# An attention and feed-forward kernel: its 32-bit transposes on half the rows of TensorE

## What is computed

```python
xn = layernorm(x)                                        # x: 32, 256, 128
q, k, v = (einsum('bsd,hde->bhse', xn, w) + b for ...)   # 16 heads of 8
scores = softmax(einsum('bhse,bhte->bhst', q, k) * scale)
att = einsum('bhst,bhte->bhse', scores, v)
attention = att.reshape(b, s, 128) @ wo.T + bo
xr = mu_r * xn + (1 - mu_r) * xn_prev;  xk = mu_k * xn + (1 - mu_k) * xn_prev
r = sigmoid(xr @ W_r.T);  k_act = square(relu(xk @ W_k.T))
return x + attention + r * (k_act @ W_v.T)
```

## Time and profile before

| | us |
|---|---|
| median of 3 runs | 471.02 |
| lowest, highest | 470.27, 473.52 |
| the profiled execution | 472.43 |
| its span, first to last instruction | 469.9 |

### The profile page before, as it was taken

The page is one execution under the profiler, slowest core; times in us unless marked ns, Lnnn a source line. Parts: engine busy times, 40 slices in busy tenths (PEclk is TensorE's granted clock), DMA queues, the critical chain, the costliest instruction groups (busy, mean ns, idle before and its releaser), DMA issues.

```text
span 469.9 us, 15674 instructions
## 1 busy us (share of the span) xinstructions
PE 449.4 (96%) x5254; PEld 271.8 (58%) x5254; DVE 400.6 (85%) x824; ACT 390.7 (83%) x865; POOL 366.8 (78%) x674
## 2 busy tenths in 40 slices
PE   5598999999999999999999999999999999999996
PEld 4245665655666565666665656566656665666553
DVE  7478999988999999899998999899998999989831
ACT  2037989988988998988989899889998989898883
POOL 6568788888888888788888888888888888887321
PEclk9559999999999999999999999999999999999999
DMA  4543455544355454344554544355545444455100
GB/s 140 133 122 94 137 155 147 145 127 127 116 150 158 141 141 141 101 138 139 149 158 125 158 132 124 109 144 158 157 133 139 137 124 126 136 151 147 49 15 22
DMA packets 85836, 60.42 MB, mean 129 GB/s; under 512 B 6192, under 2 KB 73392, under 8 KB 85808
## 3 DMA queue, kind: packets, MB, share of 16 engines
q1 hardware_dynamic: 85808, 60.06, 45.0%
HBM read 29.89 MB, written 29.36 MB: 126 GB/s over the span
## 4 chain that ended last, share of the span: by engine, by line
PE 89%; DVE 4%; issue 2%; ACT 2%; DMA 1%; ACTq 0%; DVEq 0%; SPq 0%; POOL 0%; POOLq 0%
PE bank_val L605 26%; PE bank_exp L663 19%; PE bank_max L673 10%; PE misc L744 4%; PE misc L692 4%; PE misc L714 4%; PE misc L628 3%; PE misc L703 3%; PE misc L749 3%; PE misc L756 3%; PE misc L631 2%; DVE neg_max L533 2%; PE misc L726 2%; PE misc L721 1%; PE misc L613 1%
## 5 line engine op out<-in xcount | busy, mean ns | idle before, releaser
L533 DVE TENSOR_REDUCE neg_max<-bank_max 128x2 f32<-128x512 f32 x512 | 327.7, 684 | 41.5 <-PE bank_max L673 36.1
L434 ACT ACTIVATE probs<-bank_exp 128x512 f32<-128x512 f32 x504 | 272.9, 596 | 27.1 <-PE bank_exp L663 26.9
L673 PE MATMUL bank_max<-ops 48*128 48x256 bf16 x1024 | 164.1, 278 | 0.0
L663 PE MATMUL bank_exp<-ops 51*128 51x256 bf16 x1008 | 158.5, 273 | 4.6 <-issue 3.0
L605 PE MATMUL bank_val<-probs,val 128*25 128x256 f32 x2048 | 136.3, 384 | 1.4 <-ACT probs L434 1.4
L663 PEld LDWEIGHTS bank_exp<-ops 51*128 51x128 bf16 x1008 | 72.7, 95 | 71.6 <-issue 47.4
L605 PEld LDWEIGHTS bank_val<-probs,val 128*25 128x25 f32 x2048 | 50.4, 103 | 52.1 <-issue 26.1
L673 PEld LDWEIGHTS bank_max<-ops 48*128 48x128 bf16 x1024 | 75.1, 96 | 5.2
L344 POOL TENSOR_SCALAR xn<-x_in,moments,rstd 128x128 f32<-128x128 f32 x62 | 49.3, 803 | 0.0
L383 POOL TENSOR_TENSOR mixed_x<-mixed_x,xn_t 128x512 f32<-128x512 f32 x32 | 40.7, 1273 | 2.5
L358 POOL TENSOR_TENSOR qk_l<-qk_rest,qk_m 128x512 bf16<-128x512 f32 x31 | 36.1, 1164 | 2.5
(11 more groups left out here) (73 smaller groups left out, 619.5 us busy)
## 6 DMA issues: line engine op xcount, KB each, us to landing
ops<-spill SPq DMA_DIRECT2D x128, 192.0 KB, 3.4
spill<-qk_h SPq DMA_DIRECT2D x64, 192.0 KB, 3.4
spill<-qk_m SPq DMA_DIRECT2D x64, 128.0 KB, 1.9
x_in<-x SPq DMA_DIRECT2D x32, 128.0 KB, 2.2
spill<-qk_l SPq DMA_DIRECT2D x32, 128.0 KB, 1.8
y_out<-y SPq DMA_DIRECT2D x32, 128.0 KB, 1.9
ops<-shift SPq DMA_DIRECT2D x128, 6.0 KB
w<-weights SPq DMA_DIRECT2D x1, 448.0 KB, 3.0
```

What stands on the lines that cost most here:

```text
L434: nc.scalar.activation(probs[g % 2][:, u % G, :, :], exp_bank(u, live)[:, :, :], ACT.Exp, scale=SCALE).then_inc(exp_done[u], 1)
L533: nc.vector.tensor_reduce(out=neg_max[hf][:, :, r, pr], in_=bank_max[MAX_BANK[v]][:, :, :], axis=AX_X, op=ALU.max, negate=True).then_inc(m ...
L663: exp_mm = nc.tensor.matmul(exp_bank(u, live)[:, i, :], ops[p][rows, hf, 1, pr, i * P:(i + 1) * P], ops[p][rows, hf, 0, pr, :], start=True ...
L673: max_mm = nc.tensor.matmul(bank_max[MAX_BANK[v]][:, i, :], of[rows, max_hf, 0, max_pr, i * P:(i + 1) * P], of[rows, max_hf, 1, max_pr, :] ...
```

## The change

Three groups of fp32 transposes (tokens, xn, att) are cut in two: the lower 64 rows of the data and an identity of 64 x 64 give 64 columns in `misc[:, 0]`, the upper 64 rows give 64 columns in `misc[:, 1]`. Each group has twice as many matmuls, alternating between the halves. The two banks are now one tensor of two banks; the tokens lie in the second half of both, and so do xn and att. As each group writes both banks, and no two engines may use one bank at a time, the readers and writers wait for more: the gate's Tanh for the tokens, VectorE's `inv_den` for the Tanh, the xn_t copy for ffn, xn and att, L613 for xn_t as well as att_t.

Waits of TensorE are drawn forward, ahead of the gate (the second `qk_rest`, `projected`), ahead of the gate's second matmul (`mixed`) and ahead of the ffn matmuls (`xn`, `att`). VectorE makes `inv_den` and `att` behind u = 4 instead of u = 5. ScalarE copies `att_t` behind u = 8 instead of u = 7 and `projected` behind u = 12 instead of u = 11. The rows of the output weights are permuted to the new order of `att`.

```diff
-        misc = [psum(f"misc{i}", [P, 2 * S]) for i in range(2)]
+
+        misc = psum("misc", [P, 2, 2 * S])
...
                         act.wait_ge(gate_psum, n(0))
+                        after(act, tokens_psum[0], n(-1))
+                        after(act, tokens_psum[1], n(-1))
                         after(act, ffn_done, n(-1))
 
                         nc.scalar.activation(gate[:, :], near[:, 0:S], ACT.Tanh, scale=0.5).then_inc(gate_done, 1)
...
+                    if u == 7 and (live(3) or live(-1)):
+
+                        after(act, ffn_psum, n(0))
+                        for r in range(2):
+                            after(act, xn_t_psum[r], n(3))
+                            after(act, att_t_psum[r], n(-1))
                     if u == 7 and live(3):
-                        act.wait_ge(xn_t_psum, n(3))
-                        nc.scalar.copy(xn_t[(c + 3) % TURN][:, 1:1 + S], near[:, S:2 * S]).then_inc(xn_t_done, 1)
-                    if u == 7 and live(-1):
-                        act.wait_ge(att_t_psum, n(-1))
+                        nc.scalar.copy(by_rows_of_tokens(xn_t[(c + 3) % TURN][:, 1:1 + S]),
+                                       misc[:, :, S:S + P].rearrange("p r (n c) -> p r n c", c=RG)).then_inc(xn_t_done, 1)
+                    if u == 8 and live(-1):
                         after(act, wo_psum, n(-2))
-                        nc.scalar.activation(att_t[:, :], far[:, 0:S], ACT.Identity,
+                        nc.scalar.activation(by_rows_of_tokens(att_t[:, :]),
+                                             misc[:, :, S + P:2 * S].rearrange("p r (n c) -> p r n c", c=RG), ACT.Identity,
                                              bias=col[:, C_BV:C_BV + 1]).then_inc(att_t_done, 1)
...
-                    if u == 11 and live(-1) and live(0):
+                    if u == 12 and live(-1) and live(0):
...
-                    if u == 5 and live(-1):
-                        dve.wait_ge(tokens_psum, n(-1))
-                        nc.vector.reciprocal(inv_den[:, :], by_head[:, :, E]).then_inc(inv_done, 1)
+                    if u == 4 and live(-1):
+                        dve.wait_ge(tokens_psum[0], n(-1))
+                        dve.wait_ge(tokens_psum[1], n(-1))
+                        after(dve, gate_done, n(0))
+                        nc.vector.reciprocal(inv_den[:, :, :], by_head[:, :, :, E]).then_inc(inv_done, 1)
                         dve.wait_ge(inv_done, n(-1))
-                        after(dve, att_t_psum, n(-2))
-                        nc.vector.tensor_tensor(att[:, :, :], by_head[:, :, 0:E],
-                                                inv_den[:, :].unsqueeze(2).broadcast_to([P, ST * H, E]),
+                        after(dve, att_t_psum[0], n(-2))
+                        after(dve, att_t_psum[1], n(-2))
+                        nc.vector.tensor_tensor(att[:, :, :, :].rearrange("p k r e -> p r k e"), by_head[:, :, :, 0:E],
+                                                inv_den[:, :, :].unsqueeze(3).broadcast_to([P, 2, H, E]),
                                                 ALU.mult).then_inc(att_done, 1)
...
                     if u == 3 and live(0):
                         pe.wait_ge(shift_done[1], n(0))
+                        after(pe, qk_rest_done[0], n(2))
+                        after(pe, wo_done, n(-2))
                         for i in range(ST):
+                            if i == ST - 1:
+
+                                after(pe, mixed_done, n(-1))
                             last = nc.tensor.matmul(near[:, i * D:(i + 1) * D],
                                                     mixed_x[p][:, 0, i * P:(i + 1) * P], w[:, W_R, :],
                                                     start=True, stop=True)
                         last.then_inc(gate_psum, 1)
                     if u == 3 and live(-1):
-                        pe.wait_ge(mixed_done, n(-1))
-                        after(pe, qk_rest_done[0], n(2))
-                        after(pe, wo_done, n(-2))
+                        if not live(0):
+                            pe.wait_ge(mixed_done, n(-1))
+                            pe.wait_ge(wo_done, n(-2))
+                            pe.wait_ge(att_t_done, n(-2))
                         for st in range(ST):
                             for i in range(2):
-                                k = ST * st + i
-                                last = nc.tensor.transpose(far[:, k * P:(k + 1) * P],
-                                                           mixed[:, i, st * P:(st + 1) * P], ident[:, :])
-                        last.then_inc(tokens_psum, 1)
+                                k = S + (ST * st + i) * RG
+                                for r in range(2):
+                                    rows = slice(RG * r, RG * (r + 1))
+                                    last = nc.tensor.transpose(misc[:, r, k:k + RG], mixed[rows, i, st * P:(st + 1) * P],
+                                                               ident[rows, rows])
+                                    if st == ST - 1 and i == 1:
+                                        last.then_inc(tokens_psum[r], 1)
...
+                    if u == 7 and live(3):
+                        pe.wait_ge(xn_done, n(3))
+                        after(pe, qk_rest_done[0], n(2))
+                        after(pe, qk_rest_done[1], n(2))
+                    if u == 7 and live(-1):
+                        pe.wait_ge(att_done, n(-1))
...
                     if u == 7 and live(3):
-                        pe.wait_ge(xn_done, n(3))
-                        after(pe, qk_rest_done[1], n(2))
                         for i in range(ST):
-                            last = nc.tensor.transpose(near[:, S + i * P:S + (i + 1) * P], xn[:, i, :], ident[:, :])
-                        last.then_inc(xn_t_psum, 1)
+                            for r in range(2):
+                                rows, k = slice(RG * r, RG * (r + 1)), S + i * RG
+                                last = nc.tensor.transpose(misc[:, r, k:k + RG], xn[rows, i, :], ident[rows, rows])
+                                if i == ST - 1:
+                                    last.then_inc(xn_t_psum[r], 1)
                     if u == 7 and live(-1):
-                        pe.wait_ge(att_done, n(-1))
                         for st in range(ST):
-                            last = nc.tensor.transpose(far[:, st * P:(st + 1) * P],
-                                                       att[:, st * H:(st + 1) * H].rearrange("p k e -> p (k e)"),
-                                                       ident[:, :])
-                        last.then_inc(att_t_psum, 1)
+                            for r in range(2):
+                                rows, k = slice(RG * r, RG * (r + 1)), S + P + st * RG
+                                of = att[rows, st * HALF:(st + 1) * HALF].rearrange("p k r e -> p (k r e)")
+                                last = nc.tensor.transpose(misc[:, r, k:k + RG], of, ident[rows, rows])
+                                if st == ST - 1:
+                                    last.then_inc(att_t_psum[r], 1)
...
                         after(pe, att_t_done, n(-1))
+                        after(pe, xn_t_done, n(3))
```

More of the change, by code:

```diff
@@ L120, in split_attention_ffn_kernel @@
         mixed = sb("mixed", [P, 2, S])
-        inv_den = sb("inv_den", [P, ST * H])
-        att = sb("att", [P, ST * H, E])
+        inv_den = sb("inv_den", [P, 2, H])
+        att = sb("att", [P, H, 2, E])
         att_t = sb("att_t", [P, S])
@@ L156, in split_attention_ffn_kernel @@
         tables_in = sem("tables_in")
-        xn_done, xn_t_psum, xn_t_done = sem("xn_done"), sem("xn_t_psum"), sem("xn_t_done")
+        xn_done, xn_t_done = sem("xn_done"), sem("xn_t_done")
+        xn_t_psum = [sem(f"xn_t_psum{r}") for r in range(2)]
         qk_psum = [sem(f"{a}_psum") for a in "qk"]
@@ L176, in split_attention_ffn_kernel @@
         mix_psum = [sem(f"mix_psum{g}") for g in range(NG)]
[L177 removed]
+        mixed_done, tokens_psum = sem("mixed_done"), [sem(f"tokens_psum{r}") for r in range(2)]
         inv_done, att_done = sem("inv_done"), sem("att_done")
[L179 removed]
+        att_t_done, wo_psum = sem("att_t_done"), sem("wo_psum")
+        att_t_psum = [sem(f"att_t_psum{r}") for r in range(2)]
         wo_done = sem("wo_done")
@@ L333, in step @@
                     pool.wait_ge(rstd_done, n(3))
-                    after(pool, xn_t_psum, n(2))
+                    after(pool, xn_t_psum[0], n(2))
+                    after(pool, xn_t_psum[1], n(2))
                 if live(2):
@@ L556, in step @@
                         after(dve, xn_t_done, n(3))
+                        after(dve, att_t_done, n(-1))
                         after(dve, rest_done, n(-1))
@@ L587, in _ @@
             for _ in range(WARM):
-                nc.tensor.matmul(misc[0][:, 0:P], ident[:, :], ident[:, :], start=True, stop=True)
```

(1 more changed line is left out.)

21 lines of the change are left out of this document (12 added, 9 removed).

## The result

The changed kernel took **483.72 us** (median of 4 runs, 483.32 to 485.23) beside 472.27 us for the kernel before (4 runs, 470.27 to 474.20): ratio 1.025, 95% interval 1.022 to 1.028. It is slower by 11.5 us, where 3.1 were forecast, and outside the range. Its profiled execution took 483.97 us, span 482.2.

A forecast was written before the change was run, and what follows sets the result against it. TensorE, busy 96% of the span, was taken as the bound. 24 plain steps gave +1.8 us, five first steps of loop turns +1.75, the last three -0.5: +3.1, so 474.1 us, range 466.5 to 482.

The forecast's parts named there:

- Price of a pair: TensorE: a lower and an upper half transpose run side by side, 0.056 us a pair, at most 0.11.
- slower rival: Half transposes on TensorE do not overlap, 0.11 us a pair, giving 483.5 us; chance 0.15 for 478 to 485.
- ffn's wait for att: TensorE ahead of the ffn matmuls: att, made one reduce earlier, is ready with 0.24 us of cover; costs nothing.
- The xn_t copy and the maxima: ScalarE's copy waits for the last att pair, and the maxima transposes (L613) for att_t and xn_t; exp 11 shifts +0.02 us.
- Of 0.16, 0.02 is left: Of the 0.16 us gained at xn and att, 0.02 was to survive until the maxima transposes (L613).
- projected: ScalarE's copy one unit later delays the exponential of unit 13, which exp 15 needs: shift +0.075 us a plain step.
- Gate and tokens: Gate starts 0.27 to 0.29 us later, waiting for qk_rest; tokens gain 0.16; exp 5's slack leaves nothing of either.
- First steps of loop turns: VectorE's qk_rest is later there, so the gate waits and exp 4 slips: 0.35 us each, five times, 1.75.
- the last three: Last three steps have no maxima behind att_t and keep 0.16 us each: -0.5 us.
- Sum: Plain steps 1.8 us, first steps of loop turns 1.75, last three steps -0.5: together +3.1 us.
- faster: Rival: the waits are hidden and the transposes' gain survives, 466.4 or 461.7 us; chance 0.18 for 461 to 467.
- no change: Rival: late projected is absorbed and VectorE is earlier at the loop turns' first steps, 471 us; chance 0.15.

The follow-up runs named there:

- e6: Kernel before, whole 128-row transposes kept, given the changed kernel's waits and places: 485.87 us, ratio 1.028.
- e3: Changed kernel with the waits ahead of the ffn matmul reordered so that att's is passed last, on the matmul itself: 480.38 us, ratio 1.017.
- e10: Changed kernel; projected behind unit 11, att's wait last before ffn, qk_rest's wait at gate's second matmul, one wait instead of five at xn_t copy: 474.05 us, ratio 1.004.
- e1: Changed kernel with ScalarE copying projected behind unit 11 again, as before the change: 479.77 us, ratio 1.015.
- e9: Changed kernel with two edits: projected copied behind unit 11 again, and att's wait passed last ahead of the ffn matmul: 477.19 us, ratio 1.011.
- e2: Changed kernel with the gate's first matmul waiting for shift alone, its second for qk_rest, projected and mixed: 482.68 us, ratio 1.021.
- e4: Changed kernel with the xn_t copy's five waits reordered, the one for the last att pair on the copy itself: 480.83 us, ratio 1.016.
- e12: The 474.05 us kernel with four edits (e10), with the att_t copy moved from ScalarE to VectorE behind unit 7's reduce: 482.81 us, ratio 1.021.

## Why the prediction failed, step by step

**Price of a pair: right.** Between the starts of the first and second xn pair lie 0.11, between those of att 0.06; the scores follow with no change of tile size. Last gate product to exp 4 fell from 0.645 to 0.505, last ffn product to exp 8 from 0.64 to 0.50: 0.14 a group (forecast 0.16). The Trainium skill's page "TensorE: Matmul & The Clock Gate", section "LDWEIGHTS (loading the stationary operand)", gives a load of 128 columns 0.107 us, however few rows it has, and as an estimate from that a pair would cost 0.107. The trace disagrees for these transposes: a load's row lasts 0.14, with 64 rows as with 128, but pairs follow each other at 0.06. The slower rival's 483.5 us is close to the measured time by luck and is not confirmed by it: its cause, pairs that don't overlap, is absent, and e6, which has no pairs at all, is slower still.

**ffn's wait for att: the step that failed first.** It was priced at nothing, with a cover of 0.24, and it cost 0.082. The cover was there: in e3 ffn's load stands 0.25 behind the end of att and loses nothing. But in the changed kernel the way from att's end to that load takes 0.33. What I had left out is that waits ahead of an instruction are passed one after the other, and that att's was passed with two more wait instructions behind it. e3 shows it: order alone gives it back.

**The xn_t copy and the maxima: mechanism right, size off.** "Of 0.16, 0.02 is left" should have been -0.09: 0.138 gained, 0.228 lost from exp 8 to the maxima (0.235 behind exp 9, 0.007 less ahead of it; forecast 0.14). Of that, 0.075 is the same cause on ScalarE: the copy starts 0.155 behind the last att pair, not the 0.08 that I took from copies with one wait. e10, with one wait, is at 1.344 and so 0.084 better. The rest, 0.15, is what stays in e10. I put it down to the copy's wait for both banks, which the forecast had; no run takes that wait away, the timelines alone show it.

**projected: mechanism right, 0.098 for 0.055.** ScalarE's rows stand as forecast (copy 0.50 and exponential of 13 0.75 behind that of 12, forecast 0.48 and 0.75; its end 1.37 behind for 1.34). 0.07 appears at exp 15 and 0.03 more ahead of the projections, for which I had nothing and have no reason shown; e1 takes both away. Not all of it reaches the step: taken away it gives 0.026 in e1, where ffn's wait for att takes back 0.054, and 0.061 with ffn's order mended (e9 against e3).

**Gate and tokens: right.** The gate comes 0.17 later behind exp 3, its stretch is 0.17 shorter, net nothing; e2 shows that taking the wait away brings nothing. That it was 0.17 and not 0.27 goes with projected: in e1, where that copy stands in its old place, it is 0.27 (0.582 for 0.308), and in the changed kernel exp 3 itself comes 0.10 later, which comes off the wait.

**First steps of loop turns: too low, 0.38 over a plain step on average** (forecast 0.35 - 0.075 = 0.275) at four of the five. The first of the five cost 1.2 more than a plain step, the step that leaves the loop 0.8 more, and the last three, forecast at -0.5, cost +0.55. None of this is explained.

**Sum.** 29 plain steps at 0.288 are 8.4 where the sum had 2.2: 6.2 of the 9.2 us by which the profiled spans missed it (12.3 for 3.1). The other 3.0 lie at the start, the turns and the end. Of the 0.21 a step too little, the row of waits ahead of ffn and the xn_t copy has 0.16, projected 0.04, the tile gain 0.02. The rivals "faster" and "no change" fall with it; I had given them together twice the chance of the slower one, though all three waits had a side on which they could only grow.

## What to carry to other kernels

When a change saves stream time on the busiest engine but adds semaphores to it, count the waits by number and order, not only by what they wait for: place the last-arriving one so that it rides on the instruction, and wait only for the one that implies the others. Splitting a result over two banks makes each of its readers wait for the whole of what shares them; here, at xn and att, that used up the gain. And where other engines are nearly as busy as the bound (here 83 and 85% beside 96%), a stretch shortened on one comes back at the next point where another delivers (exp 5, exp 11), so each gain has to be followed to such a point before it is summed.

## What was not expected of the hardware

- A row of waits costs by the place of the late one. att's end to ffn's first load: 0.33 us with two more wait instructions behind att's, and in e3 0.25, with nothing lost. On ScalarE, end of the transposes to the copy: 0.155 with five semaphores, 0.11 with five in e4's order and with three in e6, 0.07 with one. TensorE's wait instructions in the trace last 0.05 each and stand some 0.11 apart.
- Pairs of half transposes (64 x 64, lower and upper rows) run at 0.06 a pair in the stream, whole ones of 128 x 128 at 0.11 each; going from products of 128 rows to them costs 0.09 (0.205 from the last gate product to the first of them, for 0.11 between whole ones).
- The time of the start-up varies by more than the edits explain (profiled executions, one for each kernel): the eighth gate stands at 144.59 before, 147.97 after, 142.85 in e1, 144.51 in e3. The granted clock of the first 60 us was 0.80, 0.74 and 0.86 in the first three; but e12 had 1.00 and its start-up was no shorter. This stays open, as does the step that leaves the loop (13.39 before, 14.47 after, 14.59 in e1, 13.42 in e10).
